# Issuing the probability-times-value products of two steps together, in both attentions of a two-layer kernel

## What is computed

```python
# layer 0
raw    = einsum('bhid,bhjd->bhij', q, k)
scores = alpha * tanh(raw / beta) + lam * hamming[:, None] + lat   # hamming, lat: products of tanh features
attn   = softmax(where(causal, scores, -inf))
out    = einsum('bhij,bhjd->bhid', attn, v)
# layer 1
attn   = softmax(where(causal, einsum('bqhd,bkhd->bhqk', rope(q), rope(k)) / 4, -inf))
out    = einsum('bhqk,bkhd->bqhd', attn, v)
```

## Time and profile before

| | |
|---|---|
| median of 3 executions | 4458.54 us (4456.73 to 4461.19) |
| the profiled execution | 4471.63 us, span of its instructions 4469.8 us |
| PE busy over the span | 3854.6 us (86%) |
| ACT busy over the span | 3432.6 us (77%) |
| DVE busy over the span | 2840.0 us (64%) |
| attention of layer 0, first tanh to last exp | about 316 to 2494 us |
| attention of layer 1, first exp to last exp | about 3032 to 4151 us |
| mean granted TensorE clock | 0.959 of full speed |

### The profile page before, as it was taken

How to read it: one execution, slowest core, us unless ns; L and a number is a source line. 1 busy time by engine, 2 the same in 40 slices (tenths; PEclk the granted TensorE clock), 3 DMA queues, 4 the chain that set the end, 5 groups by cost and what they waited for, 6 DMA issues and landing times. The chain is left out here.

```text
span 4469.8 us, 66988 instructions
## 1 busy us (share of the span) xinstructions
PE 3854.6 (86%) x21966; PEld 1406.6 (31%) x21966; DVE 2840.0 (64%) x5324; ACT 3432.6 (77%) x3144; POOL 450.8 (10%) x407
## 2 busy tenths in 40 slices
PE   6958888888888888888888776758999999999787
PEld 2422222222222222222222463432222222222465
DVE  5637777777777777777777796872233332332588
ACT  2429999999999999999999412337999999999333
POOL 3520000000000000000000124650000000000133
PEclk9979999999999999999999888988999999999899
DMA  5851111112111112111111345562222222222332
GB/s 174 260 175 53 48 52 39 42 48 57 43 52 42 42 49 56 44 50 41 39 56 30 115 141 155 169 187 77 72 73 60 79 66 71 75 58 65 98 92 85
DMA packets 307816, 360.48 MB, mean 81 GB/s; under 512 B 56590, under 2 KB 237934, under 8 KB 307249
## 3 DMA queue, kind: packets, MB, share of 16 engines
q1 hardware_dynamic: 307508, 356.62, 27.4%
HBM read 228.15 MB, written 128.25 MB: 80 GB/s over the span
## 5 line engine op out<-in xcount | busy, mean ns | idle before, releaser
L835 DVE SCALAR_TENSOR_TENSOR att_prob<-att_tanh,alpha,ps 128x512 f32<-128x512 f32 (+3 forms) x2560 | 1569.5, 661 | 525.4 <-ACT att_tanh L775 333.9
L716 PE MATMUL ps<-att_q,att_k 99*128 99x512 bf16 (+7 forms) x5120 | 1196.7, 355 | 173.6 <-DMA att_v<-v_ones 79.1
L743 PE MATMUL ps<-att_prob,att_v 128*32 128x512 f32 (+3 forms) x10240 | 1215.1, 547 | 10.2 <-ACT att_prob L785 5.3
L775 ACT ACTIVATE att_tanh<-ps,rbeta 128x2048 f32<-128x2048 f32 (+3 forms) x640 | 1102.9, 1723 | 123.3 <-PE ps L716 123.3
L781 ACT ACTIVATE att_prob<-ps 128x1024 f32<-128x1024 f32 (+3 forms) x1280 | 1051.9, 920 | 78.4 <-PE ps L716 70.1
L785 ACT ACTIVATE att_prob<-att_prob 128x2048 f32<-128x2048 f32 (+3 forms) x640 | 1065.6, 1665 | 52.1 <-DVE att_prob L835 49.6
L725 PE MATMUL ps<-att_f,att_g 75*128 75x512 bf16 (+3 forms) x2560 | 854.0, 361 | 177.9 <-DVE att_prob L835 153.3
L716 PEld LDWEIGHTS ps<-att_q,att_k 96*128 96x128 bf16 (+1 forms) x5120 | 396.8, 99 | 1045.4 <-ACT att_prob L781 430.4
L823 DVE TENSOR_TENSOR att_prob<-att_prob,keep 128x256 f32<-128x256 f32 x512 | 211.5, 423 | 647.3 <-ACT att_prob L781 642.2
L725 PEld LDWEIGHTS ps<-att_f,att_g 75*128 75x128 bf16 x2560 | 235.7, 97 | 1060.8 <-DVE att_prob L835 1029.1
L743 PEld LDWEIGHTS ps<-att_prob,att_v 128*32 128x32 f32 x10240 | 202.5, 108 | 391.8 <-issue 147.2
(11 more groups left out here) (132 smaller groups left out, 2470.9 us busy)
## 6 DMA issues: line engine op xcount, KB each, us to landing
att_k<-k_parts SPq DMA_DIRECT2D x768, 64.0 KB
att_q<-q_parts SPq DMA_DIRECT2D x768, 64.0 KB
v_ones<-proj_vs SPq DMA_DIRECT2D x128, 256.0 KB, 3.1
att_v<-v_ones SPq DMA_DIRECT2D x128, 256.0 KB
post_o<-o_t SPq DMA_DIRECT2D x40, 512.0 KB, 5.1
att_f<-f_parts SPq DMA_DIRECT2D x384, 48.0 KB
o_t<-att_on SPq DMA_DIRECT2D x512, 32.0 KB, 1.9
q_parts<-proj_parts SPq DMA_DIRECT2D x32, 384.0 KB, 4.1
```

What stands on the lines that cost most here:

```text
L716: mm = pe.matmul(ps[:, bank, off:TG], keys, q_s[:, n % QU, h, off:TG], start=True, stop=True)
L743: mm = pe.matmul(ps[VW * h:VW * (h + 1), O0 + n % 2, off:TG], v_s[:, c % KU, kb % CB, h * VW:(h + 1) * VW], prob[:, S % R, h, off:TG], sta ...
L775: th.done(act.activation(tanh_s[:, S % 2, :, off:TG], ps[:, QK0:QK0 + HQ, off:TG], ACT.Tanh, scale=kn["rbeta"][:, 0:1]))
L835: sc.done(dve.scalar_tensor_tensor(prob[:, S % R, h, off:TG], tanh_s[:, S % 2, h, off:TG], kn["alpha"][:, 0:1], ps[:, E0 + h % 2, off:TG], ...
```

## The change

In the loop that writes PE's order, `weigh` is now issued in odd rounds only, and there for two steps, S-3 and S-2. In even rounds it isn't issued at all. Nothing else is changed: the same instructions run, with the same waits attached.

```diff
@@ -748,7 +748,8 @@
             for S in range(N + LAG):
                 if layer == 1 and S + 1 < N:
                     scores(S + 1, 0)
-                if S >= LAG:
+                if S % 2 == 1 and S > LAG:
+                    weigh(S - LAG - 1)
                     weigh(S - LAG)
                 if layer == 0 and S < N:
                     extra(S, 0)
```

## The result

The changed kernel takes 4826.06 us, median of 4 (4819.41 to 4829.10); the kernel before, in runs beside it, 4458.06 us. The ratio is 1.0822, 95% interval 1.0804 to 1.0841: 368 us slower. The forecast was 4640 (4590 to 4700). The direction held, the size was half of what came.

What follows compares the result with a forecast made beforehand. ACT was taken to set the pace of both layers, waiting on scores delayed by the doubled block. Layer 1's +105 us and layer 0's +77 made +182 on the 4458.5 us median: 4640 us, range 4590 to 4700.

Steps and rivals of the forecast that it cites:

- What bounds the kernel: Both layers: ACT sets the pace nearly everywhere; what matters is whether each exp or tanh finds its scores ready.
- The loop scores, block, scores, exp: Layer 1, full steps: this loop closes at 4.16 us for two steps, making most of layer 1's +105 us.
- the floor: Step from one weigh to the next: taken as 0.45 us, less excluded because operands must stream through.
- by little: Layer 1, full steps: ACT's wait for the prob buffers ends at 1.6, before exp(S+1, 0) would start at 1.66.
- the margin of 0.04: Layer 0, full steps: scores done at 3.57, tanh due at 3.65, so the 0.5 us delay is just hidden.
- The late exp of kb = 5: Layer 0, groups 2 and 3: a 0.70 us transpose after the delayed additions makes exp 0.5 us late, once each.
- Most of that is made up in r2: Layer 0, group end: r1's additions come 0.9 us late, mostly recovered in r2, leaving some 0.1.
- straight into it: Layer 0, r3: r0's weigh, 0.90 us more, adds directly to tanh's existing 0.34 us wait for scores.
- Even rounds give nothing back: Layer 0: emptied even rounds save no time, as tanh and the additions were not waiting for PE there.
- (a): Rival: PE limited layer 1 and pairing relieves it, some 40 us faster, 4418 us; chance 0.04.
- (b): Rival: layer 0 hides all its delay over r2 and kb = 5, only layer 1 pays, 4563 us; chance 0.15.
- (c): Rival: the block of two takes 1.99 us, breaking layer 0's margin, 4680 us, up to 4720; chance 0.17.

Runs made afterwards that it cites:

- the run with the filler that needn't wait: Changed kernel plus thrown-away PE products in layer 0's even rounds, from kb = 4 into a free output bank: 4654.43 us, ratio 1.0437 to the kernel before.
- the old order's three executions: Profiled executions with layer 0 unchanged: kernel before (4471.63 us), pairs in layer 1 only (median 4563.11), layer 1's paired products split around scores (median 4495.09).

## Why the prediction failed, step by step

**What bounds the kernel: right.** ACT sets the pace of both phases, and the loss is ACT waiting.

**Layer 1: right, and nearly to the number.** The loop scores, block, scores, exp took 4.12 us for 4.16, the phase grew by 103 for 105. The unknown step from one `weigh` to the next is 0.43 us (first pass to second 0.45, then 0.43, 0.43), below the 0.45 that I had called the floor; the floor was wrong by 0.02. One detail was wrong without a cost. I had said the added idle would be put down to scores, but the page puts 96.9 us of layer 1's idle on `weigh` (L743), that is on the wait for the `prob` buffer. In full steps that wait is hidden "by little", as forecast. Nearly all of the 96.9 us stands at the first exp of a group, a place for which my sum had no such wait. One of them, in ACT's timeline:

```profile
3597.52 2.35 ACT L782 ACTIVATE att_prob<-ps 128x768 f32<-128x768 f32 x5
3601.18 8.59 ACT L782 ACTIVATE att_prob<-ps 128x1024 f32<-128x1024 f32 x9 [1.30 <-PE ps L743]
```

It costs nothing, as the second exp there could follow 0.90 later, at 3602.08, but starts at 3602.27, when its scores are ready. So the loop through the scores still sets the time: the pair of steps from r3 on takes 3.98 us, where I had 3.95.

In 132 of the 144 full rounds exp(S+1, 0) is 0.08 to 0.14 us late. The step shown above is one of the other 12. There it follows two exps that started at 3621.82 and 0.90 later, so it could have started at 3623.63 and is 0.4 late, by a cause that the profile doesn't name ("issue"):

```profile
3621.82 1.98 ACT L782 ACTIVATE att_prob<-ps 128x1024 f32<-128x1024 f32 x2
3624.03 2.05 ACT L782 ACTIVATE att_prob<-ps 128x1024 f32<-128x1024 f32 x2 [0.23 <-issue]
```

That is no loss either, as the next exp, which closes the loop, waits for scores.

**Layer 0 at full clock: right in sum, wrong in one place.** Where the clock stayed up, the full steps keep 3.65 us, so the margin of 0.04 held. The late exp of kb = 5 shows in the step kb = 6, which takes 4.08 for 3.65 (0.43, I had 0.5), and that of kb = 3 of group 1 in kb = 4, 4.38 for 3.87 (0.51, I had 0.5); these are medians of the run with the filler that needn't wait. The end of a group pays 1.0 in groups 2 and 3 (0.8 in group 1), as forecast, but 0.76 of it is from r1's block and 0.3 from r3's. "Most of that is made up in r2" is the step that fails here: it isn't. Nor do the 0.90 us of r3 go "straight into it": the tanh behind r3 does wait 1.20 us for scores (I had 1.3; 0.34 before), but the exp of r2 no longer waits the 0.46 us that it did. That the two errors cancel is luck. In whole, +87 measured with some half clock left, against +77; the steps without half clock, by their medians, add up to +66.

**The step that failed: "Even rounds give nothing back" was as far as I went.** I gave each block 1.90 us everywhere, that is full clock everywhere, and priced the emptied even round at nothing. Its price is the clock, at the places named above. The trace of before had the hint in the last columns of the earlier trace rows, 0.97 in layer 0 against 0.99 in layer 1: half clock already occurred there, where PE is quietest. No rival in the prediction held it, so the range missed. Its size: 254 measured less 87 with the filler is 167 us, for 426 us more at half clock (568 less 142): 0.4 us lost per us. By the old order's three executions, 2162.2 to 2177.3 us with 54 to 114 us at half clock, it is 0.25. That the loss is higher here because the low clock meets the block, 2.99 us in place of 1.86 with 0.04 us of cover, fits these numbers and is an argument. The part of 167 that is due to the clock alone is not exact, as the filler has a small cost of its own.

The Trainium skill (TensorE: Matmul & The Clock Gate, Part 1: The HAM clock gate) says that TensorE's clock is held at half unless its recent activity releases it. The traces agree on the direction: taking the filler in and out moved half clock between 142 and 568 us. The same page's section "Why this matters for your kernels" warns of long idle gaps between bursts of products; here the clock fell without one, in the step shown with single gaps of 0.44 us at most and 0.78 in the two steps before it, so no reader of long gaps alone would have found it.

**The rivals.** (a), faster, didn't occur: the time saved is there (a block of two takes 1.86 where two alone take 2.00), and it shortens no loop. (b), layer 0 hides all, is refuted. (c), a block of 1.99 at full clock, is refuted too, as it takes 1.86; that a longer block breaks layer 0's margin is what happened, but by the clock, which (c) didn't hold.

## What to carry to other kernels

Moving work between rounds isn't free for the round that is emptied: see what the TensorE clock does there, and read the granted clock stretch by stretch before calling a margin safe. For a block that another engine waits behind, follow the loop that passes through it (here scores, block, scores, exp, and back through the number of PSUM banks); a better-packed engine helps nothing if that loop is the longer one. And a filler must not wait for anything the real work didn't wait for, or it tests two things at once.

## What the runs showed of the hardware that I hadn't expected

Half clock came in a step with PE at 2.59 us busy in 3.65 us by its records, with no gap above 0.44 us; with filler at 2.72 in 3.68 us it stayed away at the same place. Neither figure is a rule: in group 3 of the changed kernel PE was busy for 2.60 to 2.62 us of a step and kept full clock. The block of sixteen fp32 passes took 2.99 us where the clock was at half for most of it, 1.85 at full clock. Executions of the same code of layer 0 differ in this: layer 0 with the old order took 2177.3, 2166.4 and 2162.2 us in three kernels that share it, with 114, 71 and 54 us at half clock.
